# FFN weights quantized and turned in pieces during the attention; the last attention batch by batch in two banks; the last x1 measured by its ends

## The chip, the cores and the metric

One core of one Trainium2 chip. The metric is the device time of the kernel in microseconds; the time before is 1785.08, the median of three runs.

## The reference, cut to what matters

A gated block over x (32 batches of 256 tokens, width 512): cross attention to `ctx` with 16 heads of 32, then a feed-forward layer with fake quantization. Its weights are scaled row by row by their largest magnitude, its inputs by one maximum over all of x1.

```python
x = x + tanh(g_xattn) * mha(layernorm(x), ctx, ctx)          # Wq, Wk, Wv, Wo with biases
# feed-forward, H = 512, I = 1408
xq   = act_quant(layernorm(x), clip_x)                       # scale: sigmoid(clip) * max|.| / 127 over the whole tensor
gate = einsum('bsh,ih->bsi', xq, weight_quant(w_gate))       # scale: max|row| / 127, round, clip
up   = einsum('bsh,ih->bsi', xq, weight_quant(w_up))
h    = act_quant(silu(gate) * up, clip_down)
x = x + tanh(g_ffn) * einsum('bsi,hi->bsh', h, weight_quant(w_down))
```

## The kernel before

The tokens are 16 groups (`NG`) of two batches, 512 tokens, four tiles of 128. Each engine has its program written out; semaphores tie them. Nothing is planned by a tool: the order on each engine is the order of the calls.

**Attention, software-pipelined.** `body(i, j, ...)` on every engine projects group i (q, k, v as three products of fp16 high and low parts) while it attends group j = i - 1. On TensorE (L1336) a body is `turn_max(j)`, scores 0 and 1, then eight groups g of `score(2g+2)`, `pv(g)`, `score(2g+3)` with a q/k projection behind each; then v projections, `max_pair` (a product from which VectorE takes `key_max`), and four output projections `oproj` (L1247). A group g is 4 heads (chunk c = g // 2) of one batch (b = g % 2). `pv` (L1303) writes its sums into `obank` and waits until `norm(g-1)` on VectorE (L899) has read them; ScalarE makes the exponentials (`exps`, L667) and the high part of the result, GpSimd the low part. VectorE adds the projection to the residual (`x1_tile`), takes mean and variance, GpSimd makes the root by Newton steps (`root`, L545), and one body later VectorE spreads x1 (`x1_spread`, L960) and takes its maximum (`x1_top`).

**Queues.** All DMAs are issued by SP (L412): at the head of a body the row of maxima `mrow(j)` (L378), on which the first score waits, and the store of x1; then spills and restacking of q and k through DRAM, the transposes of the next x and ctx, and the loads of those after next. `body` stands in a loop on SP, GpSimd, ScalarE and VectorE, unrolled on TensorE.

**Between the passes.** The last body is `body(None, 15, ...)`: attention of group 15 alone. Meanwhile SP loads the three FFN weights (2.8 MB each, L452, L455). VectorE takes the row maxima of gate and up between the norms of this body (L1033), that of w_down behind it (L1062); ScalarE rounds (`weight_round`), VectorE converts to whole numbers in bf16 (`weight_int`, L977), TensorE turns 33 tiles (L1384), ScalarE and VectorE copy them out. x1 of group 15 is spread and its maximum taken, GpSimd reduces over the partitions (L619), and SX and INVX follow (L1084, L1087).

**First FFN pass** (L1418): 16 groups of 11 steps, gate and up for 128 columns each, h kept or spilled. Group 0's x is rounded (`x_round`, L770), converted, turned and copied before it. Then the overall maximum of h, and the down pass.

## Time and profile before

| | us |
|---|---|
| median of 3 runs (1782.42 to 1785.48) | 1785.08 |
| the profiled execution | 1786.49 |
| its span, first to last instruction | 1784.6 |
| TensorE busy in the span | 1622.6 (91%) |
| VectorE, ScalarE, GpSimd busy | 1296.8, 847.0, 549.1 |
| bodies of the attention, from one `mrow` to the next | 68.8 to 74.2 |
| last attention alone and what follows, up to the first gate-up matmul | 1163.4 to 1268.8 |

Times in the trace count from the start of the span. A busy share tells little here, since the stages have different limits; read the stretch, and in it what ended each wait. Matmuls are pipelined: the time shown for one is longer than the step to the next. A row that merges several instructions (x8) shows their common stretch. The clock column is the granted TensorE clock, 1.00 being 2.4 GHz and 0.50 being 1.2 GHz.

### The profile page before, as it was taken

What the parts mean: (1) busy time and instruction counts of PE and PEld (TensorE: products, weight loads), DVE (VectorE), ACT (ScalarE), POOL (GpSimd) and SP (SyncE); (2) the same over time, 40 slices, a digit from 0 to 9 for tenths busy, and PEclk for the clock granted to TensorE, in tenths of its full rate; (3) what the DMA queues carried; (4) which work ended last, traced back from release to release, by engine and by line L of the source; (5) the groups of instructions that cost most, each with busy time, mean ns of one, the idle gap of its engine ahead of it and who ended that gap; (6) DMA issues with size and microseconds to landing.
All of it is one profiled execution on the core that took longest, in us unless ns stands there. A gap on an engine that the chain in (4) does not pass through costs nothing.

```text
span 1784.6 us, 33864 instructions
## 1 busy us (share of the span) xinstructions
PE 1622.6 (91%) x11880; PEld 766.5 (43%) x11880; DVE 1296.8 (73%) x2055; ACT 847.0 (47%) x1132; POOL 549.1 (31%) x782
## 2 busy tenths in 40 slices
PE   3849999999999999999999999955899999989888
PEld 2324444444444444444444444422444444434333
DVE  6716777776876777777768767657677878778666
ACT  3224435336335344354353362336677777757440
POOL 6114234235144243242351341212000000006778
PEclk7969999999999999999999999978899999999999
DMA  6658577586596586675775864453055543017996
GB/s 192 166 133 177 143 178 163 148 187 161 141 200 147 157 190 159 172 166 164 180 166 150 181 164 105 112 178 136 32 218 197 196 176 136 24 48 287 421 409 235
DMA packets 275019, 307.58 MB, mean 172 GB/s; under 512 B 152160, under 2 KB 201312, under 8 KB 272352
## 3 DMA queue, kind: packets, MB, share of 16 engines
q1 hardware_dynamic: 274912, 306.00, 61.3%
q8 instruction: 85, 1.39, 0.3%
q14 instruction: 22, 0.18, 0.0%
HBM read 176.17 MB, written 95.94 MB: 152 GB/s over the span
## 4 chain that ended last, share of the span: by engine, by line
PE 54%; issue 25%; DMA 7%; DVE 7%; POOL 3%; SPq 2%; ACT 2%; POOLq 0%; ACTq 0%; DVEq 0%
PE bank L1316 12%; PE bank L1217 12%; PE bank L1219 11%; PE bank L1218 11%; PE spair L1298 5%; DMA x<-out_dram 4%; POOL yh L628 3%; PE spair L1273 2%; DMA stacks<-mT 1%; ACT pr L671 1%; DVE ndev L961 1%; PE bank L1208 1%; DMA hb<-in_L_ffn_w_gate_dram 1%; DVE bst L869 1%; SPq L359 1%
## 5 line engine op out<-in xcount | busy, mean ns | idle before, releaser
L918 DVE TENSOR_REDUCE mx<-spair 128x4 f32<-128x1024 f32 x256 | 301.4, 1219 | 57.5 <-PE spair L1273 56.9
L671 ACT ACTIVATE pr<-spair 128x1024 f32<-128x1024 f32 x256 | 259.5, 1021 | 138.7 <-PE spair L1298 138.7
L896 DVE SCALAR_TENSOR_TENSOR parts<-bank,bqk,parts 128x512 f16<-128x512 f32 x128 | 96.0, 750 | 203.6 <-ACT parts L660 197.9
L1414 PE MATMUL spair<-xqT,wgT 128*128 128x512 bf16 x704 | 182.4, 382 | 1.2 <-ACT xqT L784 1.2
L1414 PE MATMUL spair<-xqT,wuT 128*128 128x512 bf16 x704 | 181.7, 381 | 0.0
L1298 PE MATMUL spair<-stacks 128*128 128x256 f16 x1024 | 154.1, 277 | 18.2 <-ACT pr L671 11.6
L660 ACT ACTIVATE parts<-bank,bqk 128x512 f16<-128x512 f32 x128 | 88.0, 688 | 172.9 <-PE bank L1219 172.9
L1316 PE MATMUL bank<-pr,v 128*32 128x256 f32 x2048 | 140.3, 392 | 29.0 <-DVE o L912 24.1
L767 ACT ACTIVATE sil<-spair,gsc 128x512 f32<-128x512 f32 x176 | 118.2, 680 | 75.2 <-PE spair L1414 75.2
L553 POOL TENSOR_TENSOR nw<-rt 128x4 f32<-128x4 f32 x96 | 21.1, 220 | 419.6 <-DVE rt L864 414.6
L628 POOL TENSOR_TENSOR yh<-yh,x 128x512 f32<-128x512 f32 x64 | 134.7, 2135 | 49.1 <-DMA x<-out_dram 29.9
L538 POOL TENSOR_TENSOR cl<-cbuf,ch 128x512 f16<-128x512 f32 x64 | 77.1, 1208 | 220.3 <-ACT ch L648 220.2
L1114 DVE SCALAR_TENSOR_TENSOR hb<-spair,gsc,sil 128x512 f32<-128x512 f32 x132 | 98.7, 748 | 58.3 <-ACT sil L767 43.4
L1316 PE MATMUL bank<-pr,onesP 128*32 128x256 f32 x2048 | 137.7, 386 | 0.0
L1298 PEld LDWEIGHTS spair<-stacks 128*128 128x128 f16 x1024 | 89.3, 99 | 105.5 <-ACT pr L671 35.2
L685 ACT ACTIVATE mT<-bank 64x128 f16<-64x128 f32 x16 | 4.3, 272 | 243.5 <-PE bank L1282 243.5
L1217 PE MATMUL bank<-xT,wqT 128*128 128x512 f16 x256 | 98.3, 384 | 23.0 <-DMA xT<-xl 22.0
L543 POOL TENSOR_TENSOR xl<-xbuf,xh 128x512 f16<-128x512 f32 x64 | 82.5, 1293 | 84.0 <-ACT xh L654 84.0
L573 POOL TENSOR_TENSOR ol<-o,oh 128x256 f16<-128x256 f32 x128 | 86.3, 675 | 69.7 <-ACT oh L680 33.3
L621 POOL PARTITION_ALL_REDUCE small<-small x1 | 0.4, 351 | 348.3 <-DVE small L1150 348.3
L1414 PEld LDWEIGHTS spair<-xqT,wuT 128*128 128x128 bf16 x704 | 67.4, 98 | 86.9 <-DVE hb L1114 7.2
L1414 PEld LDWEIGHTS spair<-xqT,wgT 128*128 128x128 bf16 x704 | 67.7, 98 | 82.8 <-ACT sil L767 4.5
(175 smaller groups left out, 3337.9 us busy)
## 6 DMA issues: line engine op xcount, KB each, us to landing
stacks<-qk_spill SPq DMA_DIRECT2D x384, 128.0 KB, 4.3
qk_spill<-parts SPq DMA_DIRECT2D x64, 512.0 KB, 3.1
x<-out_dram SPq DMA_DIRECT2D x32, 1024.0 KB, 10.9
h_spill<-hb SPq DMA_DIRECT2D x10, 2816.0 KB, 9.2
xbuf<-in_x_dram SPq DMA_DIRECT2D x16, 1024.0 KB, 7.1
cbuf<-in_ctx_dram SPq DMA_DIRECT2D x16, 1024.0 KB, 6.4
xres<-in_x_dram SPq DMA_DIRECT2D x16, 1024.0 KB, 5.6
out_dram<-xres SPq DMA_DIRECT2D x16, 1024.0 KB, 4.3
```

Source lines behind the costliest of these rows:

```text
L628: pool.tensor_tensor(y[:, par, t, :], y[:, par, t, :], x2[:, par, t, :], ALU.add).then_inc(y_ready, 1)
L671: act.activation(pr[:, u % 4, :, :, :].rearrange("p a b q -> p (a b q)"), spair[u % 2][:, :, :].rearrange("p a q -> p (a q)"), ACT.Exp, sc ...
L767: act.activation(sil[:, k % 2, :], spair[k % 2][:, 0, :], ACT.Silu, scale=gsc[:, 0, t:t + 1]).then_inc(silu_done, 1)
L896: dve.scalar_tensor_tensor(out=parts[:, c, 2 * w + 1, :], in0=pj[(g + 1) % 3][:, :], scalar=bqk[:, w, c:c + 1], in1=parts[:, c, 2 * w, :], ...
L918: dve.tensor_reduce(mx[:, h:h + 2, b, :], spair[u % 2][:, :, :].rearrange("p a (q k) -> p a q k", q=KH), AX_X, ALU.max).then_inc(max_done, 1)
L1114: dve.scalar_tensor_tensor(out=h_place(n, par)[:, t * G:t * G + G], in0=spair[k % 2][:, 1, :], scalar=gsc[:, 1, t:t + 1], in1=sil[:, k % 2 ...
L1217: pe.matmul(dst, a[0], b[0], start=(k == 0), stop=False)
L1218: pe.matmul(dst, a[0], b[1], start=False, stop=False)
L1219: last = pe.matmul(dst, a[1], b[0], start=False, stop=(k == n - 1))
L1298: last = pe.matmul(spair[u % 2][:, a, kh * S:kh * S + S], kst[:, h, b * S + kh * P:b * S + kh * P + P], qst[:, h, b * S:b * S + S], start= ...
L1316: last = pe.matmul(obank[DK * a:DK * a + DK, at:at + S], onesP[:, :] if ones else v[:, 2 * b + kh, DK * h:DK * h + DK], pr[:, (2 * g + a / ...
L1414: last = pe.matmul(spair[k % 2][:, s, :], w[:, kc, t * P:t * P + P], xqT[:, par, kc, :], start=(kc == 0), stop=(kc == KC - 1))
```

## The change

- The three FFN weights are loaded, measured, rounded, converted, transposed and stored to DRAM in 15 pieces, one for each body with two groups (j = 0 to 14): 11 pieces of two 128x512 tiles of gate and up, 4 of one 128x1408 row block of w_down. The transposes are DMA transposes issued by SP. Behind the last body they are loaded back in turned form, as bf16.
- In each such body: SP stores the piece before and loads this one behind `mrow` and the store of x1, and transposes at the end; VectorE takes the maximum and scales in step g = 4 and converts in step g = 6; ScalarE rounds in steps 5 and 6.
- The loops over bodies on SP, GpSimd, ScalarE and VectorE become straight code.
- Last attention (j = 15): the eight groups run through the four chunks of batch 0, then of batch 1; odd groups use bank `pj[2]`, so that a PV waits for the norm before the last one; output projections of tiles 0 and 1 go behind groups 5 and 6.
- x1 of group 15 is not spread for its maximum: max and min of each row are taken, their larger distance from the mean is multiplied by the root.
- Group 0's x is spread before the overall maximum is known, a small activation loads the Silu table early, and its tiles are rounded, converted and turned one by one, with the two copies on two engines.

The diff, cut to its core and moved to the left:

```diff
+    wgu_dram = nc.dram_tensor("wgu_turned", [P, 2 * (w_gate.shape[0] // P), x.shape[2]], BF16, kind="Internal").ap()
+    wd_dram = nc.dram_tensor("wd_turned", [P, w_gate.shape[0] // P, x.shape[2]], BF16, kind="Internal").ap()
...
+wf = alloc(p1, "wf", [P, I], F32)
+wi = alloc(p1, "wi", [P, I], BF16)
...
+LAST = NG - 1
...
+def chunk_batch(j, g):
+    return (g % KC, g // KC) if j == LAST else (g // 2, g % 2)
+def x1_bank(j, t):
+    return pj[t % 2] if j == LAST else pj[t % 3]
+def pv_bank(j, g):
+    return pj[2] if j == LAST and g % 2 == 1 else obank
...
+    def load_piece(k):
+        wait(sp, fw_out, 16 * k)
+        if k < NPAIR:
+            for a in range(2):
+                m, t = (2 * k + a) // IC, (2 * k + a) % IC
+                sp.dma_start(piece_tile(wf, a), wgu_nat[m][:, t, :]).then_inc(fw_in, 16)
+        else:
+            sp.dma_start(wf[:, :], wd_nat[:, k - NPAIR, :]).then_inc(fw_in, 16)
+    def turn_piece(k):
+        wait(sp, fw_int, k + 1)
+        if k < NPAIR:
+            for a in range(2):
+                sp.dma_start_transpose(piece_tile(w_turned_b, a).rearrange("p (k q) -> p k q", q=P),
+                                       piece_tile(wi, a)).then_inc(fw_turned, 16)
+        else:
+            for a, b in ((0, 512), (512, 1024), (1024, I)):
+                sp.dma_start_transpose(w_turned_b[:, a:b].rearrange("p (k q) -> p k q", q=P),
+                                       wi[:, a:b]).then_inc(fw_turned, 16)
+    def store_piece(k):
+        wait(sp, fw_turned, piece_turns(k))
+        if k < NPAIR:
+            sp.dma_start(wgu_dram[:, 2 * k:2 * k + 2, :],
+                         w_turned_b[:, 0:2 * D].rearrange("p (t d) -> p t d", d=D)).then_inc(fw_out, 16)
+        else:
+            c = k - NPAIR
+            sp.dma_start(wd_dram[:, :, c * P:c * P + P],
+                         w_turned_b[:, 0:I].rearrange("p (k q) -> p k q", q=P)).then_inc(fw_out, 16)
     def body(i, j, par, more, first=False):
         mrow(j)
         if not first:
             store_x1(j - 1)
+            store_piece(j - 1)
+        load_piece(j)
         spill(i, 0)
         spill(i, 1)
         if not first:
...
         stack(i, j, 3)
         if more > 1:
             load_x(i + 2)
+        turn_piece(j)
     body(1, 0, 1, 2, first=True)
...
+    for i in range(2, NG):
+        body(i, i - 1, i % 2, 2 if i < NG - 2 else NG - 1 - i)
     mrow(NG - 1)
     store_x1(NG - 2)
+    store_piece(NG - 2)
     load_res(NG - 1)
     wait(sp, v_mm, NG * NT)
...
-    for m in range(2):
-        sp.dma_start(ffn_src[m], ffn_nat[m]).then_inc(fw_in[m], 16)
-    wait(sp, pv_mm, NG * NGR + 2)
-    sp.dma_start(ffn_src[2], ffn_nat[2]).then_inc(fw_in[2], 16)
+    sp.dma_start(x2[:, 0, :, :], og[0]).then_inc(f_in[0], 16)
+    wait(sp, fw_out, 16 * NPIECE)
+    sp.dma_start(wgT[:, :, :], wgu_dram[:, 0:IC, :]).then_inc(gate_up_in, 16)
+    sp.dma_start(wuT[:, :, :], wgu_dram[:, IC:2 * IC, :]).then_inc(gate_up_in, 16)
+    sp.dma_start(x2[:, 1, :, :], og[1]).then_inc(f_in[1], 16)
+    sp.dma_start(wdT[:, :, :], wd_dram).then_inc(down_in, 16)
     store_x1(NG - 1)
...
-    with pool.Fori(1, NG - 1) as i:
+    for i in range(1, NG - 1):
...
+    def piece_round(k, a):
+        if k >= NPAIR and a == 0:
+            return
+        wait(act, fw_inv, k + 1)
+        part = piece_tile(wf, a) if k < NPAIR else wf[:, :]
+        at = piece_cols(k)[0] + (a if k < NPAIR else 0)
+        act.activation(part, part, ACT.Identity, scale=winv[:, at:at + 1],
+                       bias=small[:, S1:S1 + 1]).then_inc(fw_round, 1)
...
+            if i is not None and g in (5, 6):
+                piece_round(j, g - 5)
...
-    with act.Fori(1, NG - 1) as i:
-        body(i, i - 1, i + 1)
-    body(NG - 1, NG - 2, None)
+    for i in range(1, NG):
+        body(i, i - 1, i + 1 if i + 1 < NG else None)
     body(None, NG - 1, None)
...
+    for t in range(NT):
+        x_spread(0, 0, 0, t)
+    act.activation(small[:, SPARE:SPARE + 1], small[:, S1:S1 + 1], ACT.Silu, scale=0.0)
     act.wait_ge(sc_step, 2)
     for t in range(NT):
-        x_round(0, 0, 0, t)
-    f_copies(0, 0)
-    act.wait_ge(colsc_ready, 1)
+        x_scale(0, 0, t)
+    wait(act, f_turned, 1)
+    act.activation(xqT[:, 0, 0:2, :].rearrange("p a e -> p (a e)"), pj[0][:, :].bitcast(BF16),
+                   ACT.Copy).then_inc(f_ready, 1)
+    act.wait_ge(sc_step, 3)
...
+    def x1_tile_ends(t):
+        wait(dve, x1_ready, LAST * NT + t + 1)
+        dve.tensor_reduce(xends[:, 0, t:t + 1], xres[:, t, :], AX_X, ALU.max).then_inc(x1_ends, 1)
+        dve.tensor_reduce(xends[:, 1, t:t + 1], xres[:, t, :], AX_X, ALU.min).then_inc(x1_ends, 1)
+    def x1_far_ends():
+        wait(dve, x1_ends, 2 * NT)
+        wait(dve, x1_mv, LAST * NT + NT)
+        dve.tensor_tensor(xends[:, 0, :], xends[:, 0, :], mv2[:, :, 0], ALU.subtract).then_inc(x1_far, 1)
+        dve.tensor_tensor(xends[:, 1, :], mv2[:, :, 0], xends[:, 1, :], ALU.subtract).then_inc(x1_far, 1)
+        wait(dve, x1_far, 2)
+        dve.tensor_tensor(xends[:, 0, :], xends[:, 0, :], xends[:, 1, :], ALU.max).then_inc(x1_far, 1)
+    def x1_top_last():
+        wait(dve, x1_far, 3)
+        wait(dve, x1_rstd, LAST + 1)
+        dve.tensor_tensor(amax2[:, LAST * NT:NG * NT], xends[:, 0, :], r2[:, :], ALU.mult).then_inc(x1_max, 1)
+    def piece_max(k):
+        a, b = piece_cols(k)
+        wait(dve, fw_in, piece_loads(k))
+        src = wf[:, 0:2 * D].rearrange("p (t d) -> p t d", d=D) if k < NPAIR else wf[:, :]
+        dve.tensor_reduce(wsc[:, a:b], src, AX_X, ALU.max, apply_absolute_value=True).then_inc(fw_max, 1)
+    def piece_scale(k):
+        a, b = piece_cols(k)
+        wait(dve, fw_max, k + 1)
+        dve.tensor_scalar(wsc[:, a:b], wsc[:, a:b], 1.0 / QMAX, None, ALU.mult).then_inc(fw_scale, 1)
+        wait(dve, fw_scale, k + 1)
+        dve.reciprocal(winv[:, a:b], wsc[:, a:b]).then_inc(fw_inv, 1)
+    def piece_int(k):
+        n = 2 * D if k < NPAIR else I
+        wait(dve, fw_round, piece_rounds(k))
+        wait(dve, fw_turned, piece_turns(k - 1) if k > 0 else 0)
+        dve.tensor_scalar(wi[:, 0:n], wf[:, 0:n], MAGIC, QMAX, ALU.subtract, ALU.min).then_inc(fw_top, 1)
+        wait(dve, fw_top, k + 1)
+        dve.tensor_scalar(wi[:, 0:n], wi[:, 0:n], -QMAX - 1.0, None, ALU.max).then_inc(fw_int, 1)
...
-        if i is None:
-            weight_scale(0, IC)
-            weight_scale(1, 2 * IC)
...
+        else:
+            for t in range(1, NT):
+                x1_tile(j, t)
+                x1_tile_stats(j, t)
+                if t < NT - 1:
+                    x1_tile_ends(t)
+            x1_measure(j)
+            x1_tile_ends(NT - 1)
+            x1_far_ends()
...
-    with dve.Fori(2, NG - 1) as i:
-        body(i, i - 1, i - 2, i + 1)
...
+    for i in range(2, NG):
+        body(i, i - 1, i - 2, i + 1 if i + 1 < NG else None)
     body(None, NG - 1, NG - 2, None)
-    dve.wait_ge(fw_in[2], 16)
-    dve.tensor_reduce(wsc[:, 2, 0:KC], ffn_src[2], AX_X, ALU.max,
-                      apply_absolute_value=True).then_inc(fw_max, 1)
-    weight_scale(2, 2 * IC + 1)
-    x1_shifts(NG - 1)
-    for t in range(NT):
-        x1_spread(NG - 1, t)
-    x1_top(NG - 1)
+    x1_top_last()
     dve.wait_ge(x1_max, NG)
     dve.tensor_reduce(small[:, M1:M1 + 1], amax2[:, :], AX_X, ALU.max).then_inc(m1_part, 1)
-    weight_int(1)
...
+    x1_shifts(NG - 1)
+    dve.wait_ge(diag_mm, 1)
+    dve.tensor_copy(csb[:, :], obank[:, :]).then_inc(colsc_ready, 1)
     dve.wait_ge(const_done, 8)
     dve.wait_ge(m1_all, 1)
     dve.tensor_scalar(small[:, SX:SX + 1], small[:, M1A:M1A + 1], small[:, SIGX:SIGX + 1], 1.0 / QMAX,
                       ALU.mult, ALU.mult).then_inc(sc_step, 1)
...
-    dve.wait_ge(fw_scale, 3)
...
-    weight_int(2)
-    down_copies()
-    for c in range(KC):
-        dve.tensor_scalar(diag[:, c, :], id32[:, :], wsc[:, 2, c:c + 1], None, ALU.mult).then_inc(diag_ready, 1)
...
     dve.wait_ge(sc_step, 3)
...
+    def first_ints():
+        for t in range(NT):
+            wait(dve, f_round, t + 1)
+            if t < NT - 1:
+                dve.tensor_scalar(xq[:, t, :], x2[:, 0, t, :], MAGIC, QMAX, ALU.subtract,
+                                  ALU.min).then_inc(f_tile_top, 1)
+                wait(dve, f_tile_top, t + 1)
+                dve.tensor_scalar(xq[:, t, :], xq[:, t, :], -QMAX - 1.0, None, ALU.max).then_inc(f_tile_int, 1)
+            else:
+                dve.tensor_scalar(xq[:, t, :], x2[:, 0, t, :], MAGIC, QMAX, ALU.subtract,
+                                  ALU.min).then_inc(f_top, 2)
+                wait(dve, f_top, 2)
+                dve.tensor_scalar(xq[:, t, :], xq[:, t, :], -QMAX - 1.0, None, ALU.max).then_inc(f_int, 1)
+        wait(dve, f_turned, 2)
+        dve.tensor_copy(xqT[:, 0, 2:4, :].rearrange("p a e -> p (a e)"), pj[1][:, :].bitcast(BF16)).then_inc(f_ready, 1)
...
     def oproj(j, t, i):
-        if t == 0:
+        if j == LAST and t < 2:
+            wait(pe, o_hi, j * NGR + KC)
+            wait(pe, o_lo, j * NGR + KC)
+        else:
             wait(pe, o_hi, j * NGR + NGR)
             wait(pe, o_lo, j * NGR + NGR)
-        if t < 3 and i is not None:
+        if j == LAST:
+            wait(pe, x1_ready, j * NT + t - 1 if t >= 2 else j * NT)
+        elif t < 3:
             wait(pe, v_ready, i * NT + 2 + t)
-        elif t < 3:
-            wait(pe, x1_ready, j * NT)
         else:
...
     def pv(j, g):
-        c, b = g // 2, g % 2
+        c, b = chunk_batch(j, g)
+        bank = pv_bank(j, g)
         wait(pe, exp_done, j * NU + 2 * g + 2, alone=True)
         if g == 0:
             wait(pe, v_ready, j * NT + NT, alone=True)
             wait(pe, mT_ready, j + 1, alone=True)
+        elif j < LAST:
+            wait(pe, norm_done, j * NGR + g, alone=True)
+        elif g == 1:
+            wait(pe, x1_ready, j * NT)
         else:
-            wait(pe, norm_done, j * NGR + g, alone=True)
+            wait(pe, norm_done, j * NGR + g - 1)
...
+            if i is None and g >= NGR - 3:
+                oproj(j, g - (NGR - 3), None)
...
-        for t in range(NT):
+        for t in range(NT) if i is not None else range(2, NT):
...
-    pe.wait_ge(x1_ready, NG * NT)
-    for m in range(3):
-        src = ffn_int[m]
-        pe.wait_ge(fw_int, m + 1)
...
     pe.wait_ge(diag_ready, KC)
...
-    pe.wait_ge(down_ready, IC)
+    pe.wait_ge(x1_ready, NG * NT)
+    def first_turn():
+        for t in range(NT):
+            if t < NT - 1:
+                wait(pe, f_tile_int, t + 1)
+            else:
+                wait(pe, f_int, 1)
+            for s in range(2):
+                dst = pj[s][:, :].bitcast(BF16)
+                for k in range(2):
+                    last = pe.transpose(dst[:, k * G + t * P:k * G + t * P + P],
+                                        xq[:, t, (2 * s + k) * P:(2 * s + k) * P + P], idb[:, :])
+                if t == NT - 1:
+                    last.then_inc(f_turned, 1)
...
-                last = pe.matmul(spair[k % 2][:, s, :], w[:, kc, t * P:t * P + P], xqT[:, par, kc, :],
+                last = pe.matmul(spair[k % 2][:, s, :], w[:, t, kc * P:kc * P + P], xqT[:, par, kc, :],
```

`wsc` and `winv` are now one row of 26 columns; `ints_place` is replaced by a buffer `hk`; gate and up are read as `w[:, t, kc * P:...]` in place of `w[:, kc, t * P:...]`, with the same shapes.

## Rows read from the trace of the kernel before

**Rows 1.** Busy time by stretch: us, busy by engine, clock, DMA share, GB/s.
```profile
1025.00:1094.00 69.00, 67.58 (x576) 32.09 (x575) 51.82 (x91) 30.04 (x45) 24.66 (x44) 1.00 0.60 138
...
1184.00:1197.70 13.70, 0.26 (x3) 0.01 (x1) 4.61 (x10) 2.10 (x3) 0.67 (x1) 0.66 1.03 376
...
1218.70:1231.00 12.30, 12.19 (x48) 4.97 (x48) 5.97 (x4) 12.30 (x18) 0.00 (x0) 0.86 0.47 195
1231.00:1268.80 37.80, 16.05 (x157) 11.63 (x157) 32.12 (x50) 27.00 (x40) 4.87 (x13) 0.71 0.30 104
...
884.00:887.50 3.50, 3.50 (x18) 1.66 (x17) 3.50 (x6) 0.86 (x2) 0.00 (x0) 1.00 0.05 14
```

**Rows 2.** Timeline of TensorE, 1173 to 1269: start, us, instruction, [idle before, releaser].
```profile
1173.82 1.07 PE L1316 MATMUL bank<-pr,v 128*32 128x256 f32 x16 [0.87 <-DVE o L912]
...
1177.58 1.07 PE L1316 MATMUL bank<-pr,v 128*32 128x256 f32 x16 [0.85 <-DVE o L912]
...
1197.72 1.94 PE L1316 MATMUL bank<-pr,v 128*32 128x256 f32 x16 [13.46 <-DVE o L912]
...
1218.68 0.38 PE L1217 MATMUL bank<-woT,oh 128*128 128x512 f16 x1 [3.02 <-ACT oh L680]
...
1265.76 1.86 PE L1400 MATMUL bank<-idb,xq 128*128 128x128 bf16 x16 [2.87 <-DVE xq L1108]
1268.80 1.89 PE L1414 MATMUL spair<-xqT,wgT 128*128 128x512 bf16 x4 [1.18 <-ACT xqT L784]
```

**Rows 3.** Timeline of ScalarE, last attention and rounding of x.
```profile
1176.33 1.02 ACT L671 ACTIVATE pr<-spair 128x1024 f32<-128x1024 f32 x1 [1.84 <-PE spair L1298]
...
1262.70 0.81 ACT L778 ACTIVATE x<-x,small 128x512 f32<-128x512 f32 x1
```

**Rows 4.** Timeline of VectorE, last attention and behind it.
```profile
1192.98 3.06 DVE L1033 TENSOR_REDUCE wsc<-hb 128x1 f32<-128x512 f32 x5 [9.60 <-DMA hb<-in_L_ffn_w_gate_dram]
...
1235.37 0.17 DVE L864 TENSOR_SCALAR rt<-ve 128x4 int32<-128x4 int32 x1
...
1246.20 0.22 DVE L1070 TENSOR_REDUCE small<-amax 128x1 f32<-128x64 f32 x1
1246.34 3.08 DVE L979 TENSOR_SCALAR w_ints<-hb 128x5632 bf16<-128x5632 f32 x1
```

**Rows 5.** Timeline of GpSimd: last operation of the root, and the all-reduce.
```profile
1238.71 0.20 POOL L563 TENSOR_TENSOR r<-rt,nw 128x4 f32<-128x4 f32 x1
1247.18 2.48 POOL L619 PARTITION_ALL_REDUCE small<-small  x1 [8.27 <-DVE small L1070]
```

**Rows 6.** Timeline of VectorE in a middle body.
```profile
1028.46 0.75 DVE L896 SCALAR_TENSOR_TENSOR parts<-bank,bqk,parts 128x512 f16<-128x512 f32 x1 [0.35 <-issue]
...
1059.59 0.45 DVE L905 STREAM_TRANSPOSE sT<-bank 128x256 f32<-128x256 f32 x1 [0.40 <-PE bank L1316]
...
1060.79 0.42 DVE L912 TENSOR_TENSOR o<-bank,rs 128x256 f32<-128x256 f32 x1
...
1073.35 2.36 DVE L918 TENSOR_REDUCE mx<-spair 128x4 f32<-128x1024 f32 x2 [1.00 <-PE spair L1273]
```

**Rows 7.** Timeline of TensorE in middle bodies: first scores, and one PV.
```profile
888.17 1.05 PE L1298 MATMUL spair<-stacks 128*128 128x256 f16 x8
...
1063.02 1.07 PE L1316 MATMUL bank<-pr,v 128*32 128x256 f32 x16
```

**Rows 8.** Timeline of SP's queue in middle bodies: x load, `mrow`, one transpose.
```profile
878.54 0.41 SPq L337 DMA_DIRECT2D xbuf<-in_x_dram  x1
886.06 0.52 SPq L380 DMA_DIRECT2D stacks<-mT  x1
...
1060.79 1.27 SPq L359 DMA_TRANSPOSE cT<-ch  x1
```

**Rows 9.** The line of `mrow` (L380), 16 DMAs: issue to landing.
```profile
DMA to landing us min/median/max: 2.0/2.1/4.7
```

**Rows 10.** The line of x's transposes (L350), 128 DMAs: issue to landing.
```profile
DMA to landing us min/median/max: 2.4/2.8/9.3
```

197 lines of the change are left out of this document (84 added, 113 removed).

## Prediction

> **What bounds the kernel now.** I read first the busy time by stretch. In a middle attention body (15 of them, some 69.5 us each) TensorE is busy 67.6 of 69 us, at full clock, while VectorE has 17 us and ScalarE 39 us free [rows 1]. Nothing can be gained there, and work put there is free as long as it stays out of TensorE's way. Then the same view after the last body: between the last output projection (1231) and the first gate-up matmul (1268.80) TensorE is busy 16 of 37.8 us, with weight turning and nothing else [rows 1, 2]. So the stretch from the first PV of the last attention (group 15) to the first gate-up matmul is bounded by a chain, and I read it engine by engine.
>
> TensorE stands still 13.46 us in it, released by `norm` on VectorE [rows 2]; but VectorE itself had stood 9.60 us on the gate weights' DMA (engines busy throughout, 376 GB/s [rows 1]), then did five maxima of them ahead of that `norm` [rows 4]. That is the wait behind the wait. Before and after this hole a group of PV lasts 3.76 us (1173.82 to 1177.58) [rows 2]. Behind the last projection come x1's statistics, the Newton root on GpSimd, the w_down maximum, spread and maximum of x1, the all-reduce, then three weight conversions, 33 turns, copies, the first x tile's rounding and turning.
>
> **The change, part by part: the tail.** I walk the new chain on the clock of the profile before.
>
> 1. The front of the last attention is as before up to the first group. PV(1) starts at 1173.7 (before 1173.82).
> 2. *Two banks.* PV(g+1) no longer waits for `norm(g)`. It still waits for the second exponential of its pair, whose scores come only after PV(g). In the trace that exponential runs from 1176.33 to 1177.35 [rows 3] and PV starts at 1177.58 [rows 2]; with 0.1 us for the signal PV could start at 1177.45. So this edit gives 0.13 of 3.76 us, not the 1.3 us that TensorE's idle 0.85 suggests: pitch 3.63. PV(5) starts at 1173.7 + 4 x 3.63 = 1188.2. The 13.46 us hole is gone, since nothing of the weights is loaded, measured or waited for here.
> 3. *Projections 0 and 1 between groups.* Group order is now all chunks of batch 0, then of batch 1, so tiles 0 and 1 can go after groups 5 and 6. One projection is 12 matmuls: 48 took 12.19 us at a mean clock of 0.86 [rows 1], at full clock 12.19 x 0.86 / 4 = 2.6 us. A PV with the pair of scores around it is 2.9 us (3.76 less the wait of 0.85) [rows 2], and the exponential (1.02) now hides under the projection. PV(6) starts at 1188.2 + 2.9 + 2.6 = 1193.7, PV(7) at 1199.2, its end is 1201.1.
> 4. `norm(7)`, high part, low part: before 3.02 us of TensorE's idle time [rows 2], the same now: 1204.1. VectorE has x1 tile 0 with its statistics and two ends ahead of it, some 2.6 us by 0.61 a reduction [rows 4] and as much for each of the others, in a slot of 3.7 us behind `norm(6)`. Projections 2 and 3: 5.2 us at full clock, 6.1 at the pace of before, where the clock was half for a while after just such a pause. I take 6: 1210.1.
> 5. From the last matmul to the guess of the roots it was 1230.9 to 1235.54 [rows 1, 4] with two x1 tiles and four statistics at 0.62 behind it; now one of each: 2.2 us, 1212.3. The root on GpSimd: 1235.54 to 1238.91 [rows 4, 5], 3.4 us: 1215.7. The ends of tile 3 and the distances lie beside it.
> 6. Before, 7.5 us went from the root to x1's overall maximum (1246.42) [rows 4, 5]: w_down's maximum, four spreads, one reduction over 2048 columns. Now one product of 4 columns and the small reduction: 0.5 us, 1216.2. From there to the all-reduce's end 3.2 us (1246.42 to 1249.66) [rows 4, 5], 1219.4; two small operations 0.4.
> 7. Group 0's spread runs early on ScalarE (its x1 has long been in memory). Four scalings at 0.77 (0.81 less the overlap) [rows 3]: 1222.9. Rounding of the last tile 0.6 us. Turn and copies took 3.04 us (1265.76 to 1268.80) [rows 2]; a quarter of the turns (0.5) and one of the two copies (1.0, the other is beside it on VectorE) remain: 1.6 with the signal. First gate-up matmul at about 1225.2; I take 1226, for waits of 0.1 that I haven't listed.
>
> Tail: 1268.8 - 1226 = **42.8 us**. Weights, csb and the activation table are out of this chain: 7.4 MB of loads (two x groups, residual, three weights) start with `norm(1)` of group 15, about 1179, and need 20 us at those 376 GB/s; they are needed at 1224. The clock starts low at the first gate-up matmuls as it did before, so that cancels.
>
> **The bodies: what is added to 15 of them.** VectorE, step g = 4: the maximum of 2 x 512 columns is 2 x 0.61 = 1.2 us [rows 4], 1.7 for the four w_down pieces of 1408, and two tiny operations of 0.2. It stands ahead of `norm(5)`. VectorE idles 0.40 ahead of `norm`, which ends at 1061.2, while PV takes it at 1063.02 [rows 6, 7]: 1.8 + 0.4 us to spare, 1.6 to 2.1 needed. Covered, narrowly for the wide pieces; if not, the excess would be TensorE's. Step g = 6: conversion of 1024 columns is 1024/5632 of 3.08 = 0.56 [rows 4] and a second pass not longer than that, behind ScalarE's rounding (0.8 each by x's scaling) [rows 3]. Key maxima 0 and 1 are queued behind it, then `norm(7)`; the idle 1.00 ahead of the next key maxima [rows 6] takes the 1 us up. The wide pieces come some 0.4 us late at one maximum: 4 x 0.4 = 1.6 us. On ScalarE 0.8 us goes ahead of an exponential whose product is due 2 us later.
>
> SP gets, at the end of each body, two transposes (1.27 us of issue each; three for w_down) [rows 8], at the start a store, a wait for its landing, one or two loads. Behind that wait are the spill of q/k chunk 0, which waits for its own data anyway for about as long, and the stacks, due a body later. Behind the transposes is the row of maxima, `mrow`, and that one has no slack at all: issued at 886.06, landed 2.1 later, scores at 888.17 [rows 7 to 9]. Before it SP has 7.1 us free behind the last x load (878.54), the transposes take 2.5 to 3.8 of it, and DMA engines are idle from 884 to 887.5 (share 0.05) [rows 1, 8]. Transposes are issued back to back elsewhere, so one costs the engines no more than its 1.27 us: 2.5 us in a slot of 3.5, 3.8 for the wide ones. I take 0 to 0.3 us a body, 2 us in all.
>
> Loops on four engines become straight code. The trace shows 0.35 us of "issue" at the head of VectorE's looped body [rows 6], mostly hidden; between 0 and 13 x 0.35 = 4.6 us gained, I take 2. Sum of the bodies: 1.6 + 2 - 2 = **+1.6 us**, bounds -4.6 and +14.
>
> The Trainium skill, "Runtime: NRT & Kernel Launch", Instruction fetch mechanics, says that a taken branch to a page outside the window stalls on a fetch, while straight code is fetched ahead. By that rule straight code would win back more than I take, up to the bound above; the trace shows only the 0.35 us.
>
> **Rivals.** *A, the forecast*: 1786.5 (span 1784.6 and 1.9 around it) - 42.8 + 1.6 = 1745.3 against the profiled run; that run is 1.4 above the median of three, so 1743.9.
>
> *B, the transposes hold up `mrow`.* They are queued behind the 1 MB x load. In body 0, where three loads of 1 MB had been issued 5 us ahead, `mrow` landed after 4.7 instead of 2.1 us [rows 9], so a queued transfer does pass on. If the transposes need 1 us more than the slot, each body pays it: +14 us, 1758. The Trainium skill, "DMA: Bandwidth & Descriptors", Two DMAs through the same engine are not ordered, says that within a queue of one engine descriptors start in order. That is this mechanism, and the 4.7 us agree.
>
> *C, slower.* The same place, other price: transposes have landed as late as 9.3 us after issue [rows 10]. Issued by 881.5 they would land at 890.8, and a `mrow` that can't pass them lands 2.7 us late; with the wide pieces or VectorE's norms late too it is over 3. It decides at (42.8 + 3.6)/14 = 3.3 us a body; at 3.6 the time is 1792. Against it: their median is 2.8 us [rows 10], and the slot is empty.
>
> *D, faster than A.* Straight code gives the whole 4.6 us, projections 2 and 3 run at full clock, waits are shorter: 1736.
>
> *E, it does only half.* If in the last attention the clock fell, as after the hole, every group would cost 2 us more: 10 us in the tail, 1754. Against it: at a pause of 0.85 in 3.76 us half a PV took 1.07 us, the full clock's time, and only behind the hole 1.94 [rows 2]; TensorE is busier now.
>
> **How the numbers follow.** A 0.62, B 0.17, C 0.04, D 0.10, E 0.05, and 0.02 for a result within 0.2% (3.6 us, about what a measurement of this kernel can tell from no change). Predicted time: 1744. A's own range is 1739 to 1750. To hold 8 in 10 I go to D's 1736 and to B's 1758, which takes in the bounds of the bodies. Faster 0.94, same 0.02, slower 0.04.
>
> **What would show it.** First gate-up matmul some 41 us earlier (near 1227, if bodies cost 1.6). No TensorE idle above 3.5 us between the first PV of group 15 and the last projection. PV pitch in groups 2 to 5 near 3.6, released by ScalarE's exponential and not by `norm`; a pitch of 3.0 would refute step 2. Bodies of 69.4 to 69.7 us; if they are 70.5 and scores wait for the row DMA, it is B, and if PV waits for `norm` in step g = 5, the maximum on VectorE wasn't covered. x1's maximum released by the root on GpSimd, not by the ends. From the first gate-up matmul to the end no difference: the loops there are the same. I'd be wrong altogether if bodies grew by 3 us.

## The result, and the profile after

The kernel after takes 1752.96 us (median of four runs, 1749.94 to 1756.16), the kernel before 1784.79 in the same comparison: a ratio of 0.9824, 95% interval 0.9804 to 0.9844, so 32 us or 1.8% less. The prediction was 1744, with a range of 1736 to 1758. The profiled execution is the longest of the four, 1756.16, with a span of 1754.4 against 1784.6 before.

The 30.2 us between the spans fall into four parts, taken from the issue of the row of maxima `mrow` (line 416 after, 380 before) and the first gate-up matmul:

| stretch | before | after | difference | predicted |
|---|---|---|---|---|
| start to `mrow(0)`, the same code in both | 114.48 | 117.07 | +2.6 | 0 |
| `mrow(0)` to `mrow(15)`, 15 bodies | 1048.96 | 1058.03 | +9.1 | +1.6 |
| `mrow(15)` to the first gate-up matmul | 105.36 | 64.04 | -41.3 | -42.8 |
| first gate-up matmul to the end | 515.80 | 515.26 | -0.5 | 0 |

The first line isn't shown to be an effect of the change: over the 12 kernels of this study made from the kernel after (itself included) it lies between 114.7 and 118.3. The kernel before and the one made from it have 114.5 and 114.4, though, and what sets it wasn't tried.

**The tail** went nearly as the prediction walks it. The timeline of TensorE (start, us, instruction, [idle before, releaser]), answering to [rows 2]:

```profile
1195.15 1.07 PE L1427 MATMUL bank<-pr,v 128*32 128x256 f32 x16 [0.68 <-ACT pr L735]
...
1198.74 1.07 PE L1427 MATMUL bank<-pr,v 128*32 128x256 f32 x16 [0.68 <-ACT pr L735]
...
1209.17 1.07 PE L1427 MATMUL bank<-pr,v 128*32 128x256 f32 x16
...
1214.15 0.38 PE L1319 MATMUL bank<-woT,oh 128*128 128x512 f16 x1 [3.04 <-ACT oh L744]
...
1220.80 0.38 PE L1321 MATMUL bank<-woT,ol 128*128 128x512 f16 x1
...
1239.14 1.49 PE L1523 MATMUL spair<-xqT,wgT 128*128 128x512 bf16 x3 [1.37 <-ACT xqT L864]
```

PV starts every 3.59 us and is released by ScalarE's exponential, no longer by `norm`. The hole of 13.46 us is gone; the longest idle time is the 3.04 us in which the last group is normed. Then the timelines of VectorE and, in the second fence, of GpSimd, answering to [rows 4, 5]:

```profile
1223.21 0.17 DVE L931 TENSOR_SCALAR rt<-ve 128x4 int32<-128x4 int32 x1
...
1227.04 0.22 DVE L1171 TENSOR_REDUCE small<-amax 128x1 f32<-128x64 f32 x1
...
1232.87 0.21 DVE L1177 TENSOR_SCALAR small<-small 128x1 f32<-128x1 f32 x1 [4.88 <-POOL small L683]
```

```profile
1226.53 0.20 POOL L627 TENSOR_TENSOR r<-rt,nw 128x4 f32<-128x4 f32 x1
1232.38 0.38 POOL L683 PARTITION_ALL_REDUCE small<-small  x1 [5.65 <-issue]
```

The root ends at 1226.73 and x1's maximum is there at 1227.26, but the all-reduce, itself 0.38 us, begins only at 1232.38. GpSimd stood idle for 5.65 us before it and waited for no other engine ("issue"): a new wait, where before stood 8.27 us of waiting for the maximum and a slow all-reduce. The view of the all-reduce's line shows what GpSimd's sequencer had issued at the head of this wait, two instructions of 11 ns; in the kernel before they stand right behind the root too, at 1238.8 us, 7.5 us ahead of the maximum. The first row is of the kernel after, the second of the kernel before:

```profile
L683 POOLq MODIFY_POOL_CONFIG  x2: 11/11/11, 1226.7 to 1226.7; - x2
```

```profile
L619 POOLq MODIFY_POOL_CONFIG  x2: 11/11/11, 1238.8 to 1238.9; - x2
```

**The bodies** grew by 0.2 us each where two tiles of gate and up are converted (69.8 against 69.6), and by 1.7 to 2.0 where one of the first three w_down blocks is (1.0 for the fourth, in the last of the 15 bodies). SP's timeline shows the former three as steps of 71.33 to 71.40 us between rows of maxima:

```profile
962.55 0.49 SPq L416 DMA_DIRECT2D stacks<-mT  x1
...
1033.88 0.51 SPq L416 DMA_DIRECT2D stacks<-mT  x1
...
1105.28 0.51 SPq L416 DMA_DIRECT2D stacks<-mT  x1
```

Inside one of them the timelines of VectorE, GpSimd and TensorE, a fence for each:

```profile
1077.58 1.32 DVE L1074 TENSOR_SCALAR wi<-wf 128x1408 bf16<-128x1408 f32 x1 [1.08 <-ACT wf L779]
1078.94 1.48 DVE L1076 TENSOR_SCALAR wi<-wi 128x1408 bf16<-128x1408 bf16 x1
1080.34 2.34 DVE L986 TENSOR_REDUCE mx<-spair 128x4 f32<-128x1024 f32 x2
```

```profile
1076.18 1.34 POOL L607 TENSOR_TENSOR xl<-xbuf,xh 128x512 f16<-128x512 f32 x1
...
1078.12 1.91 POOL L643 TENSOR_TENSOR xres<-xres,tgbo 128x512 f32<-128x512 f32 x1
```

```profile
1082.73 0.40 PE L1379 MATMUL spair<-parts 32*128 32x256 f16 x8 [1.04 <-DVE mx L986]
...
1086.62 0.40 PE L1379 MATMUL spair<-parts 32*128 32x256 f16 x8 [0.79 <-DVE mx L986]
```

Two passes over 1408 columns take 2.80 us. At the rate of [rows 4], where one over 5632 columns takes 3.08, the first would take 0.8, yet it takes 1.32, and GpSimd's residual beside them takes 1.91 us, where it elsewhere takes 1.27. The key maxima behind them start that much later, and TensorE, which in the middle bodies of before never stood for them, stands 1.83 us. That is the excess of a wide body.

The landings of `mrow` and of x's transposes, answering to [rows 9] and [rows 10]:

```profile
DMA to landing us min/median/max: 2.0/2.1/5.0
```

```profile
DMA to landing us min/median/max: 2.4/2.8/10.0
```

The medians are what they were. The transposes don't hold up the row.

### The profile page after: what moved, and what is told of

Same layout as the page of the kernel before. It is cut to its first block, busy times and chain, and to the rows that moved or that the text cites. A ratio compares the mean times of both kernels' runs of the same rounds, so it can differ in the third digit from the quotient of the medians.

```text
span 1754.4 us, 31208 instructions
## 1 busy us (share of the span) xinstructions
PE 1605.3 (92%) x11700; PEld 755.6 (43%) x11748; DVE 1314.4 (75%) x2097; ACT 829.7 (47%) x1110; POOL 556.9 (32%) x782
## 4 chain that ended last, share of the span: by engine, by line
PE 46%; issue 26%; DVE 12%; ACT 6%; DMA 6%; POOL 3%; SPq 2%; POOLq 0%; ACTq 0%; DVEq 0%
PE bank L1319 10%; PE bank L1427 10%; PE bank L1321 9%; PE bank L1320 9%; PE spair L1404 5%; DVE mx L986 5%; DMA x<-out_dram 4%; POOL yh L692 3%; ACT pr L735 2%; PE spair L1379 2%; ACT wf L779 1%; DVE bst L936 1%; DVE wi L1074 1%; PE bank L1310 1%; DVE rs L977 1%
## 5 line engine op out<-in xcount | busy, mean ns | idle before, releaser
L1404 PE MATMUL spair<-stacks 128*128 128x256 f16 x1024 | 153.8, 277 | 16.8 <-ACT pr L735 10.5
L637 POOL TENSOR_TENSOR ol<-o,oh 128x256 f16<-128x256 f32 x128 | 91.4, 714 | 62.5 <-ACT oh L744 32.4
```

What stands on the lines that cost most here:

```text
L1404: last = pe.matmul(spair[u % 2][:, a, kh * S:kh * S + S], kst[:, h, b * S + kh * P:b * S + kh * P + P], qst[:, h, b * S:b * S + S], start= ...
```

## Experiments

Two questions stood open: where the bodies' 9 us come from (VectorE's conversions, or SP's queue as in rival B), and what the 5.65 us ahead of the all-reduce are. Then the parts of the tail were tried one by one. All kernels start from the kernel after, but for the one that starts from before. The table has what the traces show: the 15 bodies, the last attention up to the guess of x1's root (`rt<-ve` on VectorE), from there to the first gate-up matmul, and the time. The times of warm_late, one_pass, root_dve, both, both_hold and all_four are medians of four or five executions, those of hold, thin, spread_last, straight, one_bank and proj_end come from one. They were taken in several rounds, in which the median of the kernel before was 1784.8 to 1787.1.

Two places of the traces differ between kernels whose code there is the same, and small differences have to be read beside them. The first body takes 74.2 us in before and 74.8 in after, against 72.4 to 73.3 in all others. And behind the 3.04 us pause of the last attention TensorE's clock falls to half in after, hold, thin, one_bank and both_hold, while it stays full in warm_late, one_pass, root_dve, spread_last and both.

| kernel | bodies | to the guess | to gate-up | time |
|---|---|---|---|---|
| before | 1048.96 | 71.9 | 33.4 | 1784.79 |
| after | 1058.03 | 48.1 | 15.9 | 1752.96 |
| warm_late | 1056.49 | 47.3 | 22.2 | 1759.66 |
| one_pass | 1045.75 | 47.5 | 16.2 | 1742.08 |
| hold | 1047.66 | 48.0 | 16.0 | 1745.15 |
| thin | 1044.45 | 47.9 | 15.6 | 1740.51 |
| root_dve | 1056.26 | 47.2 | 11.1 | 1747.59 |
| spread_last | 1056.53 | 46.9 | 15.7 | 1752.11 |
| straight (from before) | 1044.95 | 71.7 | 33.4 | 1782.75 |
| one_bank | 1056.40 | 49.8 | 15.5 | 1755.38 |
| both | 1046.60 | 47.1 | 11.5 | 1740.42 |
| both_hold | 1044.97 | 47.9 | 11.5 | 1738.92 |
| proj_end | 1056.79 | 46.0 | 16.0 | 1753.08 |
| all_four | 1045.24 | 46.4 | 11.5 | 1736.43 |

### The second pass of the conversion

```diff
-dve.tensor_scalar(wi[:, 0:n], wf[:, 0:n], MAGIC, QMAX, ALU.subtract, ALU.min).then_inc(fw_top, 1)
-wait(dve, fw_top, k + 1)
-dve.tensor_scalar(wi[:, 0:n], wi[:, 0:n], -QMAX - 1.0, None, ALU.max).then_inc(fw_int, 1)
+dve.tensor_scalar(wi[:, 0:n], wf[:, 0:n], MAGIC, QMAX, ALU.subtract, ALU.min).then_inc(fw_int, 1)
```

> The kernel after without the second pass of each piece's conversion (the clip at -128, which changes no value here, since every weight lies within 127 scales). Theory (the bodies' 9 us are VectorE's time: two passes over 1408 columns take 2.80 us beside a busy GpSimd and make the first maxima late, for which TensorE waits 1.83 us): the wide bodies fall from 71.35 us to about 70.2, the narrow ones from 69.8 to 69.6 to 69.8, TensorE's waits for the maxima in a wide body go from 1.83 us to under 0.6, and the time to about 1748 (1746 to 1750). Rival (the bodies wait for the pieces' transfers and transposes on SP's queue): the periods stay within 0.1 us of what they are and the time stays at 1753.

Measured: 1742.08 us, ratio to before 0.9761 (0.974 to 0.9782), more than expected. The wide bodies take 69.82 us, the narrow ones 69.38. TensorE's waits for the maxima in a wide body are down to 0.4 us, as the waits of TensorE between 1034 and 1105 show (us in total, times, longest):

```profile
PE spair L1377 <- DVE mx L986: 0.4, 1, 0.4
```

So the pieces cost mainly what VectorE's work costs, not what their transfers do; rival B is out, since the transfers and transposes are all in place. The narrow bodies fell below the 69.6 of before, which no theory had: see the straight code below.

### The same pieces, with next to no work of the engines

In `piece_max`, `piece_round` and `piece_int` only 64 columns are treated, so that the weights are not quantized:

```diff
-n = 2 * D if k < NPAIR else I
+n = 64
```

> The kernel after with maximum, rounding and conversion of each piece cut to 64 columns; the rest of the integers is a constant 1, filled in at the start. So the weights are not quantized, while every load, transpose and store of the pieces stays. Theory (the engines' work on the pieces, VectorE's above all, is what made the bodies longer): all bodies come to 69.6 us and the wide ones too, 8 us less in all, time about 1745. Rival (it is the transfers, the transposes on SP's queue or the place of the row of maxima behind them): the wide bodies stay at 71.3 us, time about 1752.

Measured: nearly all bodies at 69.36 to 69.42 us, narrow and wide alike (1044.45 in all), with every load, transpose and store in place. The transfers cost nothing that shows. The groups of VectorE's instructions (busy us, mean ns of one) hold a surprise:

```profile
L1075 DVE TENSOR_SCALAR wi<-wf 128x64 bf16<-128x64 f32 x15 | 16.2, 1082 | 0.6 <-ACT wf L780 0.6
...
L1077 DVE TENSOR_SCALAR wi<-wi 128x64 bf16<-128x64 bf16 x15 | 9.4, 625 | 0.5
```

64 columns take 1.08 and 0.63 us, about as long as 1024 did, which were 1.06 and 0.78 us. The timelines of GpSimd and of VectorE in one of the bodies tell why:

```profile
1064.46 1.34 POOL L608 TENSOR_TENSOR xl<-xbuf,xh 128x512 f16<-128x512 f32 x1
...
1065.76 0.68 POOL L638 TENSOR_TENSOR ol<-o,oh 128x256 f16<-128x256 f32 x1
```

```profile
1064.75 1.11 DVE L1075 TENSOR_SCALAR wi<-wf 128x64 bf16<-128x64 f32 x1
...
1065.89 0.59 DVE L1077 TENSOR_SCALAR wi<-wi 128x64 bf16<-128x64 bf16 x1
```

The first pass ends at 1065.86, GpSimd's instruction at 1065.80; the second at 1066.48, GpSimd's next at 1066.44. VectorE's conversion waits for the running GpSimd instruction to end.

### GpSimd held while VectorE converts

```diff
+if g == 6 and j < LAST:
+    wait(pool, fw_int, j + 1)
 if g > 0:
     o_low(j, g - 1)
```

> The kernel after, with GpSimd made to wait in each body, ahead of its low part of group 5, until the piece's conversion is done. It changes no work, only what runs beside the two passes. Theory (VectorE and GpSimd hinder each other while both work on SBUF): the two passes over 1408 columns take about 0.9 and 0.5 us (in a line through 0.43 and 0.29 us for 512 columns and 3.08 and 1.63 us for 5632) instead of 1.32 and 1.48. Rival (the passes are slow for another reason, the transfers that run beside them or the buffer they read): they stay at 1.3 and 1.5 us. The time says little: up to 4 us less if the theory holds and GpSimd's later work has room, and more where it has none.

Measured: the groups of conversions,

```profile
L1078 DVE TENSOR_SCALAR wi<-wi 128x1024 bf16<-128x1024 bf16 x11 | 4.7, 428 | 0.4
L1076 DVE TENSOR_SCALAR wi<-wf 128x1408 bf16<-128x1408 f32 x4 | 3.6, 894 | 4.9 <-ACT wf L781 4.9
L1078 DVE TENSOR_SCALAR wi<-wi 128x1408 bf16<-128x1408 bf16 x4 | 2.1, 527 | 0.1
```

0.89 and 0.53 us, against the 0.9 and 0.5 expected and the 1.32 and 1.48 of after. The same instructions and the same transfers, only GpSimd is out of the way. A wait added on GpSimd makes the kernel faster: bodies of 69.5 and 70.0 us, 1745.15 us. Both passes are still there, so it is the neighbour that costs and not the second pass as such: without the first body the bodies are 2.3 us longer than with no pieces at all (straight, below), where after's are 10.7. The first pass of the narrow pieces still takes 1.07, since it starts ahead of the held instruction: in one body GpSimd's low part of x ends at 790.42 and the pass, begun at 789.91, at 790.98, so it took 0.56 us once it was alone, which is the prediction's figure for it. The Trainium skill, "SBUF — State Buffer", SBUF: two separate sides, says that GpSimd and a VectorE instruction in a mode that uses two ports take one shared pair of ports as an exclusive lock for a whole instruction, and that the other fully blocks; by that rule a short instruction waits for the rest of a long one, and the 64 columns that end 0.06 us behind GpSimd's agree.

### The straight code by itself

The kernel before, with its four loops over bodies written out, for instance on VectorE:

```diff
-with dve.Fori(2, NG - 1) as i:
+for i in range(2, NG - 1):
     body(i, i - 1, i - 2, i + 1)
```

> The kernel before with the loops over the attention bodies on SyncE, GpSimd, ScalarE and VectorE written out as straight code (TensorE's are so already); no other change. Theory (the runs without the pieces' work stand at 69.38 us a body where before stands at 69.6, because the loops' branches and register waits are gone): the bodies fall from 69.6 to about 69.4 us, some 3 us in all, time about 1782. Rival (the 0.2 us have another cause, such as the order on SP's queue): the periods stay at 69.6 us.

Measured: 69.34 to 69.46 us for nearly all bodies, 1044.95 instead of 1048.96, 4.0 us less. But 1.8 of them lie in the first body (74.18 against 72.37), and there it is the clock: between 119 and 130 us TensorE's granted clock is 0.69, 0.50 and 0.88 in before (119 to 122, to 126, to 130) and 0.66, 0.83 and 1.00 in straight, and what it falls short of full adds up to 3.4 us and 1.7. The kernel after has the same 3.4 us there, root_dve, with the same code, 1.7. So the loops give 2.2 us, in the 14 other bodies (974.78 against 972.58), which is what the prediction took. In these 14 bodies the pieces cost 983.23 - 972.58 = 10.65 us in after (10.5 to 11.2 in the five other kernels with unchanged bodies), and without the second pass 0.5.

### A second all-reduce ahead of the last root

```diff
 o_low(j, NGR - 1)
+if j == LAST:
+    pool.partition_all_reduce(small[:, WARM:WARM + 1], small[:, S1:S1 + 1], P, RMAX)
 x1_rstds(j)
```

> The kernel after, with one more all-reduce over the partitions on GpSimd, of a constant column into a spare one, put just ahead of the last square root, where GpSimd waits 9.41 us for VectorE. Theory (the 5.65 us between the root and the first all-reduce is a lead-in that the first such instruction of the kernel pays, once): the lead-in moves into that wait, the all-reduce of M1 starts within 0.3 us of the maximum and takes its 0.38 us, so the pause of VectorE ahead of line 1177 falls from 4.88 us to under 0.8, and the time from 1753 to about 1748. Rival (each all-reduce that follows other GpSimd instructions pays it again; twelve small ones of the root lie between): the pause stays at 4.9 us and the time at 1753. Third case (the lead-in is longer than the 9.41 us, or holds up the root): the root starts late and the time rises.

Measured: 1759.66 us, slower than after by 6.7 by the medians and by 4.8 by the two ratios to before (0.9851, 0.9835 to 0.9868); from the guess to the first gate-up matmul it is 6.2 us more. The timeline of GpSimd:

```profile
1220.59 0.38 POOL L677 PARTITION_ALL_REDUCE small<-small  x1 [5.96 <-issue]
1228.71 0.19 POOL L617 TENSOR_TENSOR nw<-rt 128x4 f32<-128x4 f32 x1 [7.74 <-issue]
...
1237.88 0.38 POOL L686 PARTITION_ALL_REDUCE small<-small  x1 [5.90 <-issue]
```

The theory falls, and the rival holds in a form that is worse than it said. Not only the first all-reduce pays, but each one that follows ordinary instructions, here 5.96 and 5.90 us, and the way back to ordinary instructions pays too, 7.74, of which GpSimd would have had to wait 1.3 for VectorE's guess in any case. Two MODIFY_POOL_CONFIG stand at the head of each of the three waits, at 1214.6, 1220.9 and 1232.2 us. The Trainium skill, "GPSIMD Engine Reference", 2.1 Instruction dispatch, says that the first call of a freshly loaded kernel pays some 6 us, counted from MODIFY_POOL_CONFIG; after's 1226.7 to 1232.38 agrees.

### The last root on VectorE

The last `root` is taken out of GpSimd's program and its twelve steps stand in VectorE's, behind the ends of the last tile:

```diff
 o_low(j, NGR - 1)
-x1_rstds(j)
+if j < LAST:
+    x1_rstds(j)
...
 body(None, NG - 1, NG - 2, None)
+last_root()
 x1_top_last()
```

> The kernel after with the twelve small steps of the last square root done by VectorE, behind the ends of the last tile, instead of by GpSimd; nothing else changes. The run with a second all-reduce has shown that GpSimd changes between its ordinary instructions and the all-reduce at 5.7 to 6.0 us one way and 7.7 us the other. Theory (that change is the price, and GpSimd makes it as soon as it comes to the all-reduce, not when its input is ready): GpSimd's last ordinary instruction is now the low part that ends at 1214.05, so it is ready by 1220; VectorE's root takes twelve times 0.21 us, the maximum comes at about 1227.9 instead of 1227.04, the all-reduce 0.1 to 0.3 us later, and line 1177's step at about 1228.9 instead of 1232.87: 4.0 us less, time about 1749. Rival (GpSimd makes the change only once the maximum is there): the pause stays at 4.9 us behind the later maximum, time about 1754.

Measured: 1747.59 us, ratio to before 0.9784 (0.9768 to 0.9801). VectorE, then GpSimd:

```profile
1220.17 0.17 DVE L932 TENSOR_SCALAR rt<-ve 128x4 int32<-128x4 int32 x1
...
1224.55 0.22 DVE L1198 TENSOR_REDUCE small<-amax 128x1 f32<-128x64 f32 x1
...
1225.43 0.20 DVE L1204 TENSOR_SCALAR small<-small 128x1 f32<-128x1 f32 x1
```

```profile
1224.91 0.38 POOL L684 PARTITION_ALL_REDUCE small<-small  x1 [12.21 <-DVE small L1198]
```

The maximum is there at 1224.77, the all-reduce starts at 1224.91, and VectorE no longer waits: from the guess to the first gate-up matmul it is 11.1 us instead of 15.9. VectorE's root costs 0.55 us more than GpSimd's (4.38 against 3.83 from the guess to the maximum). GpSimd makes its change when it comes to the all-reduce, ahead of the maximum (its two MODIFY_POOL_CONFIG stand at 1212.6, right behind the last low part), so nothing ordinary may stand there late.

### The ends of x1, one bank, the place of the projections

Three parts of the change to the tail, each undone by itself. First the ends: x1 spread and its maximum taken behind the root, as before.

```diff
-x1_top_last()
+wait(dve, x1_rstd, NG)
+for t in range(NT):
+    x1_spread(NG - 1, t)
+x1_top(NG - 1)
```

> The kernel after with the last group's x1 measured as the kernel before does it: behind the root four spreads (1.91 us in the trace of before) and one maximum over 2048 columns (2.29 us), no ends. Theory (GpSimd makes its change to the all-reduce ahead of its wait for the maximum, as at 1238.8 us in before, so that the change covers VectorE's 4.2 us): the maximum comes 4.1 us later, at about 1231.2, the all-reduce is ready at 1232.4 as before, and line 1177's step moves by at most 0.3 us from 1232.87: the ends brought nothing. Rival (each us of the maximum counts, as the prediction's sum has it): the first gate-up matmul comes 4.1 us later, at about 1243.2 for the same start of the last group.

Measured on VectorE and GpSimd:

```profile
1226.23 0.22 DVE L1169 TENSOR_REDUCE small<-amax 128x1 f32<-128x64 f32 x1
...
1228.22 0.21 DVE L1175 TENSOR_SCALAR small<-small 128x1 f32<-128x1 f32 x1 [1.02 <-POOL small L683]
```

```profile
1227.74 0.38 POOL L683 PARTITION_ALL_REDUCE small<-small  x1 [5.81 <-issue]
```

The root ended at 1221.93. To line 1175's step it is 6.29 us, with the ends (line 1177 of after) 6.14. The maximum came 4.0 us later and it cost 0.15: in the kernel after, measuring x1 by its ends brings next to nothing, since GpSimd's change takes as long. With the root on VectorE and that change out of the way it wasn't tried.

Then every PV in one bank:

```diff
-return pj[2] if j == LAST and g % 2 == 1 else obank
+return obank
...
-elif j < LAST:
-    wait(pe, norm_done, j * NGR + g, alone=True)
-elif g == 1:
-    wait(pe, x1_ready, j * NT)
 else:
-    wait(pe, norm_done, j * NGR + g - 1)
+    wait(pe, norm_done, j * NGR + g, alone=True)
```

> The kernel after with every PV of the last attention in one bank, so that each waits for the group before to be normed. Theory (with two banks it is the exponentials that set the pitch): the pitch of the first PVs goes from 3.59 us to the 3.76 us of before, and the first gate-up matmul comes 1.0 to 1.5 us later, measured from the last row of maxima: 65.0 to 65.5 us instead of 64.04. Rival (the second bank is what makes room for the projections and carries the gain): more than 3 us later.

Measured: the first gate-up matmul 65.26 us behind the last `mrow`, with the pitch of before:

```profile
1187.16 1.07 PE L1423 MATMUL bank<-pr,v 128*32 128x256 f32 x16 [0.85 <-DVE o L980]
...
1190.92 1.07 PE L1423 MATMUL bank<-pr,v 128*32 128x256 f32 x16 [0.85 <-DVE o L980]
```

3.76 us against 3.59, as expected. Of the 1.2 us in all, however, only 0.7 are the second bank's: from PV(1) to PV(5) it is 15.07 us against 14.36, and from PV(5) to PV(7) 10.43 in both. PV(1) itself starts 0.9 us later behind `mrow` (10.2 against 9.3), and in kernels with two banks that time lies between 9.1 and 10.4 too.

Last, output projections 0 and 1 behind the last PV:

```diff
-if i is None and g >= NGR - 3:
-    oproj(j, g - (NGR - 3), None)
...
-for t in range(NT) if i is not None else range(2, NT):
+for t in range(NT):
     oproj(j, t, i)
```

> The kernel after with output projections 0 and 1 of the last group behind the last PV instead of between the PVs, and x1's tile 0 with them. Theory (they fill time that TensorE spends on nothing else there only in part): PV(7) starts 5 us earlier, behind it four projections of 2.6 us at the full clock or 3.5 at the half one stand instead of two, and the first gate-up matmul comes 2 to 3.5 us later, at 66 to 67.5 us from the last row of maxima instead of 64.04. Rival (the order of the projections is free, since their sum is the same): within 0.7 us of 64.04.

Measured: the first gate-up matmul 61.96 us behind the last `mrow`, 2.1 us *earlier* than after's, against my theory and its rival. I had forgotten what these two wait for:

```profile
1205.38 1.07 PE L1423 MATMUL bank<-pr,v 128*32 128x256 f32 x16 [1.11 <-ACT pr L735]
...
1207.25 0.39 PE L1315 MATMUL bank<-woT,oh 128*128 128x512 f16 x1
...
1217.40 0.38 PE L1317 MATMUL bank<-woT,ol 128*128 128x512 f16 x1
```

They need only the groups of batch 0, so they run at once behind the last PV and fill the 3.04 us in which group 7 is normed. TensorE has no pause there, and its clock doesn't fall: all matmuls take 0.38, where in after those from 1215.5 to 1218.5 take 0.63. The 2.1 us mix two things. From PV(1) to the guess it is 36.0 us here and in all_four; with the projections between the groups it is 37.1 in the five kernels whose clock stays full behind the pause, and 38.8 in after, hold, thin and both_hold, where it falls. So the place of the projections gives 1.2 us by itself and 2.9 where the clock would fall, and what decides whether it falls isn't shown. In the time, from one execution (1753.08), this is not to be seen.

### What helped, together

> The kernel after with both edits that helped: one pass in each piece's conversion, and the last square root on VectorE. Theory (the two work at different places, the bodies and the stretch behind the last attention, so that their gains add): one pass gave 10.9 us and the root 5.4 us against the median of after, of which 12.3 and 5.7 us lie between the first row of maxima and the first gate-up matmul as the traces have it (bodies 1058.0 to 1045.8, tail 64.0 to 58.3): together 16 to 18 us, time about 1736 (1734 to 1739). Rival (what the one gives the other takes back, for instance because GpSimd's change still runs when the maximum comes): 1742.

One pass and the root on VectorE give 1740.42 us, ratio 0.9747 (0.9733 to 0.976). The trace has both gains whole (bodies 1046.6, the all-reduce 0.13 us behind its input), but the sum of the medians' gains, 1736.7, isn't reached; in this profile the first `mrow` is issued at 118.3, with warm_late's the latest of all kernels, and one_pass alone had it at 114.7. So 1740.42 can't be told from one_pass's 1742.08 with any certainty, and it is the stretches, not the medians, that show the root's gain.

GpSimd held in the four wide bodies as well:

```diff
+if g == 6 and NPAIR <= j < LAST:
+    wait(pool, fw_int, j + 1)
```

> The kernel with both edits, and GpSimd held ahead of its low part of group 5 in the four wide bodies until the conversion is done. Theory (a conversion beside a GpSimd instruction waits for that to end): the conversion of 1408 columns falls from 1.31 to 0.89 us, the wide bodies from 69.82 to about 69.5 us, 1 to 1.5 us less in all. Rival (the held low parts and residuals come late for the output projections or the transposes): the wide bodies stay at 69.8 us or grow.

Measured: conversions of 0.89 us instead of 1.31, the first three wide bodies at 69.40 to 69.43 us, no longer above the narrow ones; bodies 1044.97, 1.6 us less. 1738.92 us, ratio 0.974 (0.9727 to 0.9754).

And the projections behind the last PV:

> The kernel with both edits and the held GpSimd, and with output projections 0 and 1 behind the last PV. Theory (behind the last PV these two projections, which need only the groups of the first batch, fill the 3.0 us in which the last group is normed, and TensorE is spared the pause and the half clock behind it): projections end 10.3 us behind PV(7) with no idle time between, the stretch from the last row of maxima to the first gate-up matmul falls from 58.6 to 59.4 us to about 56.5, and the time to about 1736.5 (1735 to 1738). Rival (with the root on VectorE the later x1 tile 0 crowds VectorE, or the half clock comes back at another place): the stretch stays at 58.5 us or more and the time at 1739.

Measured: 1736.43 us (1731.68 to 1736.71), ratio to before 0.9706 (0.969 to 0.9722), the fastest kernel of the study, 0.9% below the kernel after by the medians and 1.2% by the two ratios to before. The stretch from the last `mrow` to the first gate-up matmul is 57.9 us, against 58.6 and 59.4 in the two before it, where 56.5 was expected: the last attention's start, before the first groups have settled, takes 1.1 us more than in after (PV(1) starts 10.4 us behind `mrow` against 9.3; in both it was 9.9, in proj_end 10.0). Where it starts after 9.1 to 9.3 us (after, hold, thin, both_hold), the first half of PV(0) took 1.2 to 1.4 us, elsewhere 1.9, the time at half clock: the full clock comes back later there. From PV(1) on the stretch is 47.5 us, 1.2 less than in both and 2.9 less than in both_hold.

## Why the prediction was right, and where it was off

The time fell into the range, but 9 us from the number. By its own steps, for the profiled runs (1745.3 predicted, 1756.2 measured): 2.6 us are in the start, 7.5 in the bodies, 1.5 in the tail, and -0.5 behind it. The forecast's own range, 1739 to 1750, didn't hold the result; the wider one did, which had been opened to 1758 for rival B, and B is not what happened. With the pieces at what they measured, 10.7 us where 3.6 were taken (1.6 for VectorE, 2 for SP), the number would have been about 1751.

**The tail, steps 1 to 7.** Shifted by 11.66 us, by which `mrow(15)` was issued later (1175.10 against 1163.44):

| event | predicted, shifted | measured |
|---|---|---|
| PV(1) starts | 1185.4 | 1184.4 |
| PV(5) starts | 1199.9 | 1198.7 |
| PV(7) starts | 1210.9 | 1209.2 |
| projection 2 starts | 1215.8 | 1214.2 |
| last projection ends | 1221.8 | 1221.2 |
| root ends | 1227.4 | 1226.7 |
| x1's maximum ends | 1227.9 | 1227.3 |
| all-reduce ends | 1231.1 | 1232.8 |
| first gate-up matmul | 1237.7 | 1239.1 |

Step 1 was off by 1.0 us, to the good: the full clock came back earlier in PV(0) than in before. Step 2 was right in size and reason: the exponential sets the pitch, 3.59 instead of 3.63, and one_bank shows 3.76 without it. Step 3 is right to 0.6 us (PV(5) to PV(7) 10.4 instead of 11.0), step 5 to 0.1, and in step 4 the pause is right and projections 2 and 3 took 7.0 us instead of 6, since the clock fell 1.4 us into them. What steps 3 and 4 didn't ask is whether the projections between the groups are worth it; proj_end says no, by 1.2 us and by 2.9 where the clock falls, for they would have covered the very pause of 3.0 us that step 4 counts.

**Step 6 is the one that failed in the tail.** It priced the all-reduce by [rows 5] at 3.2 us from maximum to end. It took 5.5. The row of before shows an all-reduce of 2.48 us behind 8.27 us of idle time, and I read the idle time as waiting for VectorE. It was that, but GpSimd's change to the all-reduce lay under it, from 1238.8 us on, and cost nothing there. The 2.48 themselves are another thing: VectorE converted weights from 1246.34 to 1249.42 [rows 4], and the all-reduce ended at 1249.66; in straight it took 2.56 and ended 0.25 behind the same conversion, and in the twelve other kernels, with no conversion beside it, it takes 0.38. So the term had the right order of size by two errors, which is luck. The tail's net 1.5 us are luck in part too: step 6 was 2.3 us short, projections 2 and 3 another 1.0, and steps 1 to 3 gave 1.7 of it back. Taking 4 us off VectorE ahead of the all-reduce uncovered what they had hidden; spread_last shows that the ends brought 0.15 us, root_dve that to take the change out of the way gives 4.8.

**The bodies: +1.6 predicted, +9.1 measured.** Of its terms,

- the maximum at step g = 4 was covered, as forecast: 1.61 us for the wide piece (1.7 predicted), no PV waited for it;
- the loops' end was right: 2.2 us for the 2 taken (straight, without the first body);
- SP's part was oversized: 2 us predicted, none measured (thin);
- the conversion was mis-sized, and this is the error. Predicted were 1.6 us, 0.4 for each of the four wide bodies and nothing for the others. Measured against straight the pieces cost 10.7 us in the 14 bodies behind the first, 1.9 in a wide one (0.9 in the fourth) and 0.4 in a narrow one; without the second pass it is 0.5, with both passes and GpSimd held 2.3. The price came from [rows 4], where GpSimd has nothing to do beside the conversion but the all-reduce, and that was what waited. In step g = 6 GpSimd has a row of instructions, and each pass waits for one of them: 1.06 and 0.78 us for 1024 columns, 1.31 and 1.33 for 1408, where [rows 4] gave 0.56 and 0.77 for the first pass. The 1.00 us of idle time [rows 6] takes up one such pass and not two.

**The rivals.** B and C are out: `mrow` lands in 2.1 us, and thin, with all transposes in place, has bodies of 69.4. D is out too: the straight code gave 2.2 us and not 4.6, and the projections behind the pause ran at half clock for some 3.3 us. E is out: the first halves of PV take 1.07 us in all groups from PV(1) on; the clock, low up to PV(0) as before, falls again only behind the pause. The time of 1753 is near E's 1754, by another road. What the prediction lacked is a rival in which VectorE and GpSimd hinder each other, though it had called VectorE's work in the bodies free.

## What to carry to other kernels

A duration holds for the neighbours that it was measured with: before pricing an instruction on VectorE by a row, look what GpSimd did beside that row and what it will do at the new place. When a wait is shortened, look what its idle time covered on the engine that was waited for; a long idle time ahead of an instruction can hide that instruction's own start. And work without inputs that are late belongs behind the last input that is early, where the next pause is, rather than where the engine happens to be idle now.

## What the runs showed of the hardware

- GpSimd needs 5.62 to 6.26 us (nine times in eight kernels) to change from ordinary instructions to the all-reduce, and took 7.74 us the one time that the way back lay open (warm_late). It is shown as idle "issue", with two MODIFY_POOL_CONFIG at its head. GpSimd makes the change when it comes to the instruction, ahead of its wait. The second all-reduce of the kernel, with nothing ordinary between it and the first, starts 0.10 us behind its input (1567.13 to 1567.23) and takes 0.35.
- A conversion on VectorE from SBUF to SBUF waits until the GpSimd instruction that runs when it starts ends: 64 columns took 1.08 us, and 1408 columns 1.31 beside GpSimd and 0.89 without. GpSimd waits the other way round: its residual took 1.91 us instead of 1.27 beside two passes. The maxima that read PSUM (1.22 us) and those of the pieces (1.21 us for 1024 columns) were not lengthened by it.
- Loops over bodies of 69 us, on four engines, cost 0.2 us a body (2.2 us in 14 bodies of straight).
- TensorE's clock can differ where the instructions around are the same: behind the same pause of 3.04 us it fell to half in five kernels and stayed full in five.
